# Differential attention of a fused transformer kernel: products on VectorE and GpSimd, against all products on VectorE

## The reference, cut to what matters

```python
q = (x @ Wq.T).reshape(b, n, H, D, 2).transpose(0, 1, 4, 2, 3).reshape(b, n, 2 * H, D) * scale   # H = 16, D = 8
k = (x @ Wk.T)...                     # likewise: 32 keys of 8 numbers in each position
v = (x @ Wv.T).reshape(b, n, H, 2 * D).transpose(0, 2, 1, 3)
att = softmax(einsum('bnqd,bnkd->bnqk', q, k))          # 32 x 32 in each position
att2 = att6[:, :, 0, :, 0, :] - lam * att6[:, :, 1, :, 1, :]   # 16 x 16
out = einsum('bnah,bhnd->bnad', att2, v)                # 16 x 16 in each position
out = _rmsnorm(out) * (1.0 - LAMBDA_INIT)
```

## Time and profile before

| what | value |
|---|---|
| three runs of the kernel before | 4079.4, 4089.78, 4094.57 us, median 4089.78 |
| span of the profiled execution, first to last instruction | 4081.4 us |
| that execution's own time | listed only as this span; it lies between the lowest and the median run |
| busy share of the span: PE, DVE, ACT, POOL | 79%, 64%, 22%, 22% |
| mean granted TensorE clock | 0.886 of full speed |
| differential attention, mixed groups | 163.8 us once, then 166.3 to 166.4 us six times |
| differential attention, last group alone | 148.2 us |

### The profile page before, as it was taken

The page is one execution under the profiler, slowest core; times in us unless marked ns, Lnnn a source line. Parts: engine busy times, 40 slices in busy tenths (PEclk is TensorE's granted clock), DMA queues, the critical chain, the costliest instruction groups (busy, mean ns, idle before and its releaser), DMA issues. The chain is left out here.

```text
span 4081.4 us, 37792 instructions
## 1 busy us (share of the span) xinstructions
PE 3229.0 (79%) x12328; PEld 1917.7 (47%) x12328; DVE 2606.1 (64%) x7724; ACT 906.7 (22%) x1774; POOL 903.3 (22%) x508
## 2 busy tenths in 40 slices
PE   6897889778896889868888788968889688986224
PEld 4555545445553555545454455535555354553112
DVE  2223487746957479564877459584695648863777
ACT  0212222123222222222222232222222122122110
POOL 0001143013420134111430124201331113401440
PEclk8898999989997999979999799978999789996657
DMA  5023111040102201031110301022010211102000
GB/s 190 26 78 124 42 57 47 10 162 11 62 31 89 83 26 62 22 124 42 52 52 10 141 32 62 31 89 83 26 62 22 105 61 42 62 8 86 0 0 6
DMA packets 76604, 236.65 MB, mean 58 GB/s; under 512 B 7888, under 2 KB 46928, under 8 KB 58352
## 3 DMA queue, kind: packets, MB, share of 16 engines
q1 hardware_dynamic: 76400, 234.04, 16.0%
HBM read 229.82 MB, written 4.19 MB: 57 GB/s over the span
## 5 line engine op out<-in xcount | busy, mean ns | idle before, releaser
L674 PE MATMUL ps<-aTA,stream 128*128 128x512 f32 x2304 | 1066.7, 614 | 23.3 <-DVE hTA L1263 23.3
L674 PEld LDWEIGHTS ps<-aTA,stream 128*128 128x128 f32 x2304 | 451.5, 198 | 538.3 <-issue 484.4
L690 PE MATMUL ps<-stream,hTA 128*128 128x256 f32 x2304 | 569.5, 404 | 95.2 <-DVE xA L1248 94.3
L690 PEld LDWEIGHTS ps<-stream,hTA 128*128 128x128 f32 x2304 | 464.3, 203 | 244.2 <-DVE xA L1248 106.7
L941 ACT ACTIVATE hTA<-ps 128x512 f32<-128x512 f32 x288 | 171.4, 595 | 1004.2 <-PE ps L674 1003.9
L254 POOL TENSOR_TENSOR work<-hTB 128x2048 f32<-128x2048 f32 x64 | 350.9, 5484 | 132.2 <-DVE sbuf L1356 78.4
L392 POOL TENSOR_TENSOR rstdB<-veB,mhalf 128x4 f32<-128x4 f32 x48 | 48.5, 1010 | 1247.3 <-DVE veB L1061 1247.3
L1356 DVE TENSOR_REDUCE sbuf<-work 128x256 f32<-128x2048 f32 x128 | 291.9, 2281 | 15.2 <-POOL work L254 13.0
L1263 DVE TENSOR_TENSOR hTA<-ps,hTA 128x512 f32<-128x512 f32 x288 | 196.3, 682 | 144.0 <-ACT hTA L941 144.0
L262 POOL TENSOR_TENSOR hTB<-pb,hTB 128x2048 f32<-128x2048 f32 x32 | 163.6, 5113 | 356.3 <-DVE pb L1388 356.3
L254 DVE TENSOR_TENSOR work<-hTB 128x2048 f32<-128x2048 f32 x64 | 196.7, 3073 | 69.3 <-ACT hTB L1002 62.7
(11 more groups left out here) (228 smaller groups left out, 5066.7 us busy)
## 6 DMA issues: line engine op xcount, KB each, us to landing
stream<-in_experts SPq DMA_DIRECT2D x72, 1024.0 KB, 6.0
stream<-in_experts SPq DMA_DIRECT2D x72, 512.0 KB, 3.9
work<-in_ctxT SPq DMA_DIRECT2D x32, 1028.0 KB, 6.7
hTB<-in_ctxN SPq DMA_DIRECT2D x32, 1024.0 KB, 7.0
ctxA<-in_ctxT SPq DMA_DIRECT2D x16, 1024.0 KB, 10.4
stream<-in_ctxT SPq DMA_DIRECT2D x16, 1024.0 KB, 10.2
xA<-in_x SPq DMA_DIRECT2D x8, 512.0 KB, 12.2
out<-xnB SPq DMA_DIRECT2D x32, 128.0 KB, 1.8
```

What stands on the lines that cost most here:

```text
L674: ins = mm(ps[:, 2 * (f % 2) + u, :], we[:, c:c + P], aTA[:, k, :], start=k == 0, stop=k == KT - 1)
L690: ins = mm(ps[:, 4, (t % 2) * D:(t % 2 + 1) * D], hE[:, (e - 1) % 2, j, t * P:(t + 1) * P], we[:, j, :], start=j == 0, stop=j == HID // P - 1)
```

## The change

GpSimd no longer makes any of the three products of a tile. VectorE makes score products 1 and 3 itself, just ahead of their reductions, and the second value product right behind the reduction of the first. The waits on GpSimd's products go; ScalarE's copy into `qkv` now waits for VectorE's second value product instead. GpSimd's generator keeps its number of steps, so the order of everything else stays.

```diff
@@ gpsimd, back() @@
-                            if i < T:
-                                pool.wait_ge(act_done, A["qkv", i])
-                                if i >= 1:
-                                    pool.wait_ge(vec_done, V["dred", i - 1, 3])
-                                qk_product(nc.gpsimd, i, 1).then_inc(pool_done, O.step("dprod", i, 1))
-                            yield
-                            yield
-                            if 1 <= i <= T:
-                                pool.wait_ge(vec_done, V["datt", i - 1])
-                                if i >= 2:
-                                    pool.wait_ge(vec_done, V["pred", i - 2, 1])
-                                pv_product(nc.gpsimd, i - 1, 1).then_inc(pool_done, O.step("pprod", i - 1))
-                            yield
-                            if i < T:
-                                pool.wait_ge(vec_done, V["dred", i, 1])
-                                qk_product(nc.gpsimd, i, 3).then_inc(pool_done, O.step("dprod", i, 3))
-                            yield
-                            yield
+                            for _ in range(5):
+                                yield
@@ scalar, qkv_copy(t) @@
                             if t >= 2:
-                                act.wait_ge(vec_done, V["pprod", t - 2])
-                                act.wait_ge(pool_done, O["pprod", t - 2])
+                                act.wait_ge(vec_done, V["pprod", t - 2, 1])
@@ vector, scores(t, c) @@
-                            if c % 2 == 0:
-                                own_steps()
-                                qk_product(vv, t, c).then_inc(vec_done, V.step())
-                                own_steps()
-                            else:
-                                v.wait_ge(pool_done, O["dprod", t, c])
+                            own_steps()
+                            qk_product(vv, t, c).then_inc(vec_done, V.step())
+                            own_steps()
@@ vector, weights(t) @@
-                            if t >= 2:
-                                v.wait_ge(pool_done, O["pprod", t - 2])
@@ vector, values(t) @@
                             output(t, 0, prod[:, 0, :])
+                            pv_product(vv, t, 1).then_inc(vec_done, V.step("pprod", t, 1))
@@ vector, mean_squares(t) @@
-                            v.wait_ge(pool_done, O["pprod", t])
+                            own_steps()
                             output(t, 1, prodV)
```

## The result

The changed kernel takes 4113.3 us (median of 13 runs, 4097.6 to 4120.9), the kernel before 4090.45 (13 runs, 4076.7 to 4099.2). The ratio is 1.0057, 95% interval 1.0043 to 1.0070: +23 us, between 18 and 29. The forecast was 4115 and +25. A later comparison, in its own set of runs, gave 1.0042 (1.0026 to 1.0058), in agreement.

The account below looks back on a forecast made before the run. VectorE was taken to set the pace of the differential attention stages: 230.4 added less 164.9 and 21.2 removed, +44.3, less 18.9 absorbed, gives +25.4 us on the 4089.8 median, 4115, range 4090 to 4160.

Parts of the forecast that it names:

- What bounds: Differential attention stages, mixed and last groups: VectorE sets the pace, busy 156.06 of 166.40 us and 137.99 of 148.20.
- The added term: VectorE in differential attention: 96 more products at 2.4 us each, 230.4 us, bounds 220 and 240.
- The removed term: VectorE's products and subtraction lose 164.9 us of stalls by GpSimd, and direct waits for GpSimd's products lose 21.2 us.
- The absorbed term: Mixed stages: VectorE's waits for silu (2.1 us) and exponentials (0.6 us) are swallowed by its later arrival, 18.9 us in all.
- The sum: Whole kernel: 44.3 net for VectorE less 18.9 absorbed, +25.4 us, giving 4115; chance 0.65, own range 4100 to 4135.
- The path: Mixed stage: VectorE some 4 us ahead after the first tile, 3 to 4 us behind at the end.
- The moved wait: ScalarE's copy into `qkv` waits for VectorE's second value product; turn held 2 us for tile 3, cost zero, at most 14.
- The unseen collision: GpSimd's power at L477, 2.9 us, beside a new VectorE product in mixed groups: taken as zero, 50 us kept for the range.
- rival 1: Mixed groups: GpSimd's power shuts out VectorE's new product to its end, +50 us, 4165; chance 0.17.
- Rival 2: Mixed groups: more is absorbed and no difference is left, each about -1 to +2 us, total 4085 to 4100; chance 0.12.
- Rival 3: Mixed stages: TensorE's slow restarts after idle time, 50 us in all, lie on the path and vanish, 4065; chance 0.06.

Follow-up runs that it names:

- doubled product: The changed kernel with the second value product made twice on VectorE, 32 products more: 4186.8 us, ratio 1.0246 to the kernel before.
- the two fast versions: Changed kernel with GpSimd making score products 1 and 3 behind VectorE's 0 and 2: 3996.3 us; with the second value product on GpSimd too: 3944.3 us.

## Why the prediction was right, step by step

**What bounds.** Right. The doubled product costs its full 2.4 us, and with no products a mixed stage drops from 170.5 to 143.1.

**The added term.** 230.4 us forecast; the stages say 219.5. That is 2.29 us per product; the 0.11 that I added for handing over does not show in this difference, since the kernel without products keeps these waits, though it does in the doubled product (2.4), which brings a wait of its own.

**The removed term.** 164.9 + 21.2 = 186.1 us forecast; 188 measured. Each of the three stalled groups of operations fell to its free duration. VectorE's busy time rose by 56.9 us, where +55 was forecast. The two measured terms are differences of whole stages, so they hold everything that was absorbed: their difference, 31 us, is already the net, and no absorbed term may be taken off it.

**The absorbed term.** 18.9 forecast: right in size, not in mechanism. The wait at the expert multiply went from 2.1 to 0.3 us in the second group and that for the exponentials vanished. The waits of the changed kernel in its second group (columns as in the earlier trace rows):

```profile
ACT hTB L984 <- DVE hTB L262: 13.7, 2, 9.5
...
PE ps L519 <- ACT oTB L873: 4.1, 3, 3.1
...
DVE hTA L1246 <- ACT hTA L925: 0.3, 1, 0.3
```

That is 2.4 us per mixed stage, 16 to 17 in all, somewhat less than I took. But I had later arrivals swallow these waits as the added products pile up, and in the kernel without any of the products, where nothing was added to VectorE, they are gone as well. Its second group has no wait for the silu and this one for the exponentials:

```profile
DVE sm L1356 <- ACT sbuf L998: 0.3, 1, 0.3
```

So they went with GpSimd's products and the stalls, and the added products met hardly any slack. The sums over the eight stages (busy us of the engines) of the kernel before, the one without products and the changed one say the same:

```profile
sum 1310.30, PE 1044.91 PEld 600.30 DVE 1228.28 ACT 239.00 POOL 605.71; mean PE 130.61 PEld 75.04 DVE 153.53 ACT 29.88 POOL 75.71
...
sum 1122.10, PE 989.94 PEld 575.93 DVE 1069.67 ACT 234.81 POOL 93.41; mean PE 123.74 PEld 71.99 DVE 133.71 ACT 29.35 POOL 11.68
...
sum 1341.70, PE 1057.73 PEld 606.93 DVE 1286.55 ACT 234.33 POOL 92.85; mean PE 132.22 PEld 75.87 DVE 160.82 ACT 29.29 POOL 11.61
```

VectorE's idle time falls from 82 to 52 us when the products go, and stays near there (55) when VectorE makes them.

**The sum.** From before to after, the stages grew by 31 us in the first pair of profiles and 29 in the second, against my +25.4: VectorE's busy time grew by 58 us in them, 3 more than my 55, and its idle time fell by 27, where my terms come to 30 (21.2 + 18.9 less 96 x 0.11). The measured total is +23 us. The forecast was thus a few us too low for the stages, and what lies outside them took some of it back, which I had put at zero; that 25 lands so close to 23 is in part luck. Two slips of the prediction changed nothing: 2.33 + 2.2 + 2.29 is 6.8, not 6.9, and the lower end of its own range, +15, is 4105, not 4100.

**The path.** The mixed stage was forecast at 168 to 171 (170.5), the last at 147 to 149 (147.9). Within the second group VectorE's first product of the second tile starts 3.8 us earlier after the stage's start than before the change, that of the third 3.7, that of the fourth 0.2, and the stage ends 4.1 us later: some 4 ahead, then 3 to 4 behind, as forecast.

**The moved wait.** The same rows: ScalarE's copy waits 13.7 us (two waits) instead of the 7.3 of the earlier trace rows, and TensorE waits 4.1 us for the turned output, where the kernel before had 1.9:

```profile
PE ps L535 <- ACT oTB L889: 1.9, 3, 1.0
```

The forecast of 2 us of delay per stage holds. VectorE has no wait for TensorE in that stage, so it stayed off the path.

**The unseen collision, rival 1.** Refuted. GpSimd's power and VectorE's new product, second group:

```profile
1065.27 2.91 POOL L461 TENSOR_TENSOR mx<-mx,mhalf 128x16 f32<-128x16 f32 x1 [63.00 <-DVE mx L1393]
```

```profile
1065.88 2.29 DVE L254 TENSOR_TENSOR work<-hTB 128x2048 f32<-128x2048 f32 x1
```

The product begins 0.6 us into the power, ends 2.29 us later and inside it. Over all 128 score products the longest is 2341 ns. That is one of three in the last group, where the prediction had the product issued first; the trace has the power 0.02 us ahead there as well, and so clears the power's first part too:

```profile
3887.57 2.91 POOL L461 TENSOR_TENSOR mx<-mx,mhalf 128x16 f32<-128x16 f32 x1 [56.36 <-DVE mx L1393]
```

```profile
3887.59 2.34 DVE L254 TENSOR_TENSOR work<-hTB 128x2048 f32<-128x2048 f32 x1
```

The Trainium skill's rule that the shared pair is kept for a whole instruction ("SBUF — State Buffer", "SBUF: two separate sides") agrees with every pair of large products here, and not with this power, if its 2.91 us in the profile are taken as its length.

**Rival 2** (nothing left, 4085 to 4100): out; the interval of the ratio (1.0043 to 1.0070) does not hold 1, though the effect is near 0.5%. **Rival 3** (TensorE's warm restarts): the slow spells exist, 5.41 against 3.7 us, but follow VectorE's pace. In the changed kernel they stayed (TensorE is busy 148.67 us in the second group's stage, 146.85 before); with shorter stages most of them went without being aimed at (142.67 and 141.67 us in the two fast versions, 138.70 without the products).

## What to carry to other kernels

Before taking work from, or giving work to, GpSimd, look for VectorE durations whose mean is far above their minimum: a stall by the other engine is booked as the duration of the blocked instruction (3417 ns on average for the subtraction, 1225 without it), not as idle time. What then decides is what stands beside GpSimd's operation: started behind VectorE's own product, beside reductions and work that reads PSUM, the same help that had cost 188 us for 219 made the kernel 3.5% faster than before, and 2.2% with the two score products alone. And don't take an engine's busy time as a floor where some of it is restarts after waits.

## What the runs showed of the hardware

Two elementwise products of 128x2048 with both inputs in SBUF exclude each other on VectorE (2.29 us) and GpSimd (4.46 us), whichever starts first. Where GpSimd's was listed 0.02 us ahead, VectorE's took 6.58 us; where VectorE's was 0.05 us ahead, GpSimd's took 6.56.

VectorE's reductions, and its multiply and accumulation that read one input from PSUM, run beside GpSimd's product without a loss that the rows show. With the score products behind VectorE's, mostly such work stood beside them: GpSimd's 64 averaged 4499 ns (5484 before) and VectorE's 128 reductions 2282.

That is not so for every VectorE operation with a single large input. Before the change GpSimd's score product 1 starts, in 22 cases, 0.11 to 0.14 us into the clamp of the scores (128x1024, one input in SBUF, two constants) and takes 4.90 to 4.94 us instead of 4.46, with 0.58 us of the clamp left:

```profile
1018.04 0.69 DVE L1365 TENSOR_SCALAR sbuf<-sbuf 128x1024 f32<-128x1024 f32 x1
```

```profile
1018.15 4.92 POOL L254 TENSOR_TENSOR work<-hTB 128x2048 f32<-128x2048 f32 x1 [7.41 <-DVE sbuf L1356]
```

The product of the earlier trace rows that starts at 3897.63, just behind such a clamp and with the same operations beside it otherwise, takes 4.46. And a scaling of 128x16 numbers by a factor per partition waits for the end of GpSimd's product (3785.82 + 4.46 = 3790.28), in the version with the score products behind VectorE's:

```profile
3789.55 0.77 DVE L1372 TENSOR_SCALAR ri<-ri,neglam 128x16 f32<-128x16 f32 x1
```

```profile
3785.82 4.46 POOL L254 TENSOR_TENSOR work<-hTB 128x2048 f32<-128x2048 f32 x1 [5.35 <-DVE work L254]
```

A power on 128x16 numbers, 2.9 us on GpSimd, does not hold up a VectorE product that begins 0.02 or 0.6 us into it (2.34 and 2.29 us).
